# Normalising the queries in channel layout, from two rows that travel through memory, in a gated delta recurrence

## The chip, the cores and the metric

The kernel runs on one core of a Trainium2 chip. The metric is the time of one execution on the device, in microseconds. The profile names the engines PE (matrix products; PEld is its weight load), DVE (VectorE), ACT (ScalarE), POOL (GpSimd) and SP (which here only issues DMAs). The engines run their own instruction streams and meet at semaphores.

## The reference

For 4 sequences of 1024 tokens and 512 features, with 16 heads of 128 channels:

```python
xn = layernorm(x)
q, k, v = xn @ Wq, xn @ Wk, xn @ Wv
beta = sigmoid(xn @ Wb + bb)
q = silu(causal_dwconv(q, qconv_w, qconv_b))      # 4 taps along the tokens
k = silu(causal_dwconv(k, kconv_w, kconv_b))
q = layernorm(q per head, qn_w, qn_b)             # over a head's 128 channels
k = layernorm(k per head, kn_w, kn_b)
S = (1 - b_t) * S + b_t * outer(v_t, k_t)         # for each token t
o_t = S @ q_t
s = (o * silu(xn @ Wg)) @ Wo
g = silu(ffn(xn))                                 # on the 512 tokens of the highest scores, 0 elsewhere
out = x + s * g
```

## The kernel before

Three stages follow each other: the tokens' layer norm and their transposes, the recurrence, and two passes over the kept tokens. The change lies in the recurrence alone, which takes some two thirds of the time.

The recurrence handles one head of one sequence at a time: 64 such units. They run in a software pipeline, in which one *step* of the program does four things: it projects unit A and convolves it, makes q and k of unit B (A's predecessor), finishes q and k of unit C (the one before), and does the chunked recurrence of unit D (the one before that). Tokens are worked in 8 chunks of 128. Each engine's order within a step is written by hand, and every wait is a semaphore with a count. Two steps make a pair (`par` 0 and 1), with small differences: the token ranks of the router are computed in DVE's gaps, one half in each (`rank_greater` in par 0, `rank_ties` in par 1), and the weights of v are loaded once for a pair.

What happens to q of one unit:

1. PE projects it into `ps_proj`, channels on partitions, tokens along the row; ACT (`tap`) and DVE (`convolve`) apply the four taps into `act_cm`; ACT applies silu in place.
2. PE transposes it chunk by chunk (`turn`, 8 transposes, name `QT`), ACT copies it to `tok[0]` with tokens on partitions (`tokens(0)`), and DVE takes the statistics over the channels from there (`statistics(0)`, `variance`). GpSimd raises the variance to the power -1/2, and DVE makes the shift (`shifts`).
3. DVE scales and shifts `tok[0]` (`normalise`: 8 instructions, one for each chunk, since rstd and shift are then one value for each partition). In the next step PE transposes it back (`QB`, 8 transposes), and ACT copies it to `q_cm` with the norm's weight and bias (`ready(0)`).

The keys go the same way, but ACT normalises them, and GpSimd weights them for the state update with two passes over 1024 columns (`k_weighted` and `k_tokens_done`), with q's weighting by the cumulated decay (`q_cum`) between the two. The first of the three waits for `dmat_done`, which DVE's scan over the decays signals. `ps_work` is two PSUM buffers that the transposes (QB, QT, KB, KT), the state updates (UP), the scores (SC) and the outputs (OUT) use in turn. For the first sequence the weights are also split into two parts by ACT and GpSimd; later sequences load the split parts again from memory.

## Time and profile before

| | |
|---|---|
| median of 3 runs | 2653.92 us (2642.51 to 2655.47) |
| the profiled execution | 2649.24 us, its span 2647.5 us |
| busy in the span | PE 2538.9 us, DVE 1779.9 us, ACT 1122.9 us, POOL 849.7 us |
| granted TensorE clock, mean | 0.987 |

An engine's busy time is an average over three stages with different limits, and a busy PE is not PE at its peak. What the change is worth is read from one step in the middle of the recurrence: from the start of an instruction to the start of the same instruction one step on. Each row of the trace gives the start, the duration, the line and the operation with the tiles written and read; a bracket behind it gives the idle time of the engine before it, and who ended it.

### The profile page before, as it was taken

How to read it: one execution, taken by the hardware profiler on the slowest of the kernel's cores; microseconds unless marked ns; L12 is line 12 of the kernel's file. 1: busy time of each engine (PE TensorE's matmuls, PEld its weight loads, DVE VectorE, ACT ScalarE, POOL GpSimd, SP SyncE). 2: the span in 40 equal slices, each digit the busy share in tenths (PEclk: the TensorE clock that was granted, in tenths of full speed). 3: DMA queues.
4: the chain of work that ended last, by engine and by line, in shares of the span. 5: the costliest groups of instructions: out<-in, count | busy, mean ns of one | idle time of the engine just before them, and what ended most of it. 6: DMA issues, size and time to landing. Idle time of an engine off the chain costs nothing. (4 is left out here: it accounts for less than half of the span.)

```text
span 2647.5 us, 44202 instructions
## 1 busy us (share of the span) xinstructions
PE 2538.9 (96%) x15744; PEld 2254.0 (85%) x15744; DVE 1779.9 (67%) x3716; ACT 1122.9 (42%) x1513; POOL 849.7 (32%) x442
## 2 busy tenths in 40 slices
PE   5899999999999999999999999997899999999997
PEld 4789889999999989999998999997788887888886
DVE  5678888888888888888888888888431222433232
ACT  5444454444444444444444444444432323322221
POOL 1245445443434334343434334344100000211220
PEclk8999999999999999999999999999999999999998
DMA  7544443643333353333354333342461101441320
GB/s 273 167 136 153 151 135 128 219 133 104 119 119 119 111 176 125 119 127 104 118 169 134 119 108 122 119 128 80 156 230 49 63 32 56 128 150 48 111 84 27
DMA packets 220876, 327.51 MB, mean 124 GB/s; under 512 B 56310, under 2 KB 156918, under 8 KB 216058
## 3 DMA queue, kind: packets, MB, share of 16 engines
q1 hardware_dynamic: 125946, 192.21, 22.2%
q10 hardware_dynamic: 86144, 109.06, 12.4%
q0 software_dynamic: 8704, 25.19, 3.1%
q8 instruction: 46, 0.75, 0.1%
q14 instruction: 36, 0.29, 0.0%
HBM read 237.77 MB, written 97.03 MB: 126 GB/s over the span
## 5 line engine op out<-in xcount | busy, mean ns | idle before, releaser
L983 DVE SCALAR_TENSOR_TENSOR xn_rows<-ps_proj,conv,xn_rows 128x1021 f32<-128x1021 f32 x381 | 488.0, 1281 | 127.8 <-ACT xn_rows L890 118.7
L1160 PE MATMUL ps_proj<-xt_hi,w_hi 128*128 128x512 f32 x1008 | 411.7, 408 | 20.1 <-DVE xn_rows L983 13.6
L1162 PE MATMUL ps_proj<-xt_hi,w_lo 128*128 128x512 f32 x1008 | 396.8, 394 | 0.0
L1161 PE MATMUL ps_proj<-xt_lo,w_hi 128*128 128x512 f32 x1008 | 395.4, 392 | 0.0
L941 ACT ACTIVATE rc_tok_k<-rc_tok_k,rc_small 128x128 f32<-128x128 f32 x512 | 204.2, 481 | 353.2 <-DVE rc_small L1017 353.2
L782 POOL TENSOR_TENSOR rc_k_state<-rc_tok_k,k_norm_rows 128x1024 f32<-128x1024 f32 x64 | 153.5, 2399 | 515.1 <-issue 397.5
L1182 PE MATMUL ps_proj<-wv_hi,xt_hi 128*128 128x256 f32 x1024 | 294.9, 288 | 0.6 <-PEq L75 0.6
L1183 PE MATMUL ps_proj<-wv_lo,xt_hi 128*128 128x256 f32 x1024 | 289.5, 283 | 0.0
L1184 PE MATMUL ps_proj<-wv_hi,xt_lo 128*128 128x256 f32 x1024 | 289.3, 283 | 0.0
L814 POOL TENSOR_TENSOR rc_small<-rc_small,rc_minus_half 128x16 f32<-128x16 f32 x64 | 187.2, 2924 | 218.9 <-DVE rc_small L1012 218.9
L890 ACT ACTIVATE xn_rows<-ps_proj,conv 128x1024 f32<-128x1024 f32 x127 | 152.9, 1204 | 231.7 <-PE rc_ps_work L1136 231.7
L1160 PEld LDWEIGHTS ps_proj<-xt_hi,w_hi 128*128 128x128 f32 x1008 | 190.6, 189 | 57.3 <-issue 15.2
L1162 PEld LDWEIGHTS ps_proj<-xt_hi,w_lo 128*128 128x128 f32 x1008 | 189.8, 188 | 42.0
L1161 PEld LDWEIGHTS ps_proj<-xt_lo,w_hi 128*128 128x128 f32 x1008 | 190.8, 189 | 35.1
L1586 DVE TENSOR_TENSOR ff_wide_lo<-ff_wide,ff_wide_hi 128x512 fp32r<-128x512 f32 x64 | 44.3, 693 | 245.2 <-ACT ff_wide_hi L1501 245.1
L1247 PE MATMUL rc_ps_work<-rc_v_beta,rc_scores 128*128 128x128 f32 x1024 | 190.6, 278 | 12.2 <-DVE rc_scores L1068 12.1
L1182 PEld LDWEIGHTS ps_proj<-wv_hi,xt_hi 128*128 128x128 f32 x1024 | 196.1, 192 | 1.0 <-issue 1.0
L1183 PEld LDWEIGHTS ps_proj<-wv_lo,xt_hi 128*128 128x128 f32 x1024 | 196.3, 192 | 0.0
L1184 PEld LDWEIGHTS ps_proj<-wv_hi,xt_lo 128*128 128x128 f32 x1024 | 196.0, 191 | 0.0
L1249 PE MATMUL rc_ps_work<-rc_states,rc_q_cum 128*128 128x128 f32 x896 | 175.6, 278 | 0.0
L1582 DVE TENSOR_TENSOR gt_wide<-gt_ps_turn,gt_gate 128x512 f32<-128x512 f32 x64 | 44.2, 691 | 194.2 <-ACT gt_gate L1494 194.2
L991 DVE BATCH_NORM_STATS2 rc_stats<-rc_tok_k 128x6 f32<-128x128 f32 x512 | 105.3, 279 | 100.3 <-ACT rc_tok_k L900 100.3
(177 smaller groups left out, 5770.9 us busy)
## 6 DMA issues: line engine op xcount, KB each, us to landing
rc_decay_all<-scratch_decay ACTq DMA_DIRECT2D x64, 512.0 KB, 3.5
rc_cum_all<-scratch_cum ACTq DMA_DIRECT2D x64, 512.0 KB, 3.6
scratch_o<-rc_o_sb ACTq DMA_DIRECT2D x64, 512.0 KB, 3.2
w_hi<-scratch_w_split SPq DMA_DIRECT2D x48, 512.0 KB, 4.0
w_lo<-scratch_w_split SPq DMA_DIRECT2D x48, 512.0 KB, 4.8
wv_hi<-scratch_wv_split SPq DMA_DIRECT2D x24, 512.0 KB, 3.9
wv_lo<-scratch_wv_split SPq DMA_DIRECT2D x24, 512.0 KB, 4.8
scratch_w_split<-w_hi SPq DMA_DIRECT2D x16, 512.0 KB, 2.8
```

Source lines behind the costliest of these rows:

```text
L782: nc.gpsimd.tensor_tensor(k_tokens[:], tok[1][:], k_norm_rows[:, 0:1].to_broadcast([P, NC, P]), ALU.mult).then_inc(S["k_weighted"], 1)
L814: nc.gpsimd.tensor_tensor(small[:, 6], small[:, 5], minus_half[:], ALU.pow).then_inc(S["rstd_done"], 1)
L941: last = nc.scalar.activation(tok[1][:, c], tok[1][:, c], ACT.Identity, bias=small[:, 7, 1, c:c + 1], scale=small[:, 6, 1, c:c + 1])
L983: nc.vector.scalar_tensor_tensor(out=act_cm[j][:, back:], in0=projected[:, 0:L - back], scalar=conv[par][:, j, t:t + 1], in1=act_cm[j][:, ...
L1160: nc.tensor.matmul(out, hi, xt_hi[:, k, cols], start=k == 0, stop=False)
L1161: nc.tensor.matmul(out, hi, xt_lo[:, k, cols], start=False, stop=False)
L1162: last = nc.tensor.matmul(out, lo, xt_hi[:, k, cols], start=False, stop=k == KC - 1)
L1182: nc.tensor.matmul(out, xt_hi[:, k, cols], wv_hi[:, k], start=k == 0, stop=False)
L1183: nc.tensor.matmul(out, xt_hi[:, k, cols], wv_lo[:, k], start=False, stop=False)
L1184: last = nc.tensor.matmul(out, xt_lo[:, k, cols], wv_hi[:, k], start=False, stop=k == KC - 1)
L1247: last = nc.tensor.matmul(out, scores[:, c], values, start=True, stop=c == 0)
L1249: last = nc.tensor.matmul(out, q_cum[:, c * P:(c + 1) * P], states[:, c - 1], start=False, stop=True)
```

## The change

q is no longer carried through token layout. Its transposes to tokens stay, but only the statistics use them: DVE takes them straight from PSUM, so ACT's copy `tokens(0)`, DVE's `normalise` and PE's transposes back (`QB`) go. In their place, rstd and shift of all 1024 tokens are stored as two rows in memory by ACT, in 4-byte pieces (each partition holds 8 tokens of each row, 128 tokens apart), and loaded back as rows that are repeated on all 128 partitions. The load stands behind the store's completion in ACT's queue. In the next step DVE multiplies q in channel layout by the one row and adds the other (`scale_q`), and `ready(0)` reads that.

```diff
                 if C_.live:
                     after_pair(dve, decay_loaded[C_.par], C_.pair)
                     ...
                     nc.vector.tensor_tensor_scan(dmat[C_.par]...).then_inc(S["dmat_done"], 1)
+                    scale_q()
+                if B_.live:
+                    statistics(0)
                 if A_.live and not first_done(A_.i):
                     convolve(0)
                 if B_.live:
-                    statistics(0)
                     statistics(1)
...
-                def normalise():
-                    after_step(dve, "shift_done", B_.i)
-                    for c in range(NC):
-                        last = nc.vector.tensor_scalar(tok[0][:, c], tok[0][:, c], small[:, 6, 0, c:c + 1],
-                                                       small[:, 7, 0, c:c + 1], ALU.mult, ALU.add)
-                    last.then_inc(S["q_normed"], 1)
+                def scale_q():
+                    after_step(dve, "q_rows_loaded", C_.i, 16)
+                    after_step(dve, "q_turned", C_.i)
+                    nc.vector.tensor_tensor(q_silu[C_.par][:], q_silu[C_.par][:], q_rows[:, 0], ALU.mult
+                                            ).then_inc(S["q_scaled"], 1)
+                    after_step(dve, "q_scaled", C_.i, 2, 1)
+                    nc.vector.tensor_tensor(q_silu[C_.par][:], q_silu[C_.par][:], q_rows[:, 1], ALU.add
+                                            ).then_inc(S["q_scaled"], 1)
...
+                def store_rows():
+                    after_step(act, "rstd_done", B_.i)
+                    after_step(act, "shift_done", B_.i)
+                        act.dma_start(row(scratch["q_rows"], B_.i).rearrange("(k c p) -> p k c", k=2, p=P),
+                                      rstd_shift[:, 0]).then_inc(S["q_rows_stored"], 16)
+                def load_rows():
+                    after_step(act, "q_rows_stored", B_.i, 16)
+                    after_step(act, "q_scaled", B_.i - 1, 2)
+                    act.dma_start(q_rows[:].rearrange("p k t -> p (k t)"),
+                                  row(scratch["q_rows"], B_.i).partition_broadcast(P)
+                                  ).then_inc(S["q_rows_loaded"], 16)
...
                 if B_.live:
-                    after_step(act, "rstd_done", B_.i)
-                    after_step(act, "shift_done", B_.i)
+                    store_rows()
                     for c in range(NC):
-                        last = nc.scalar.activation(tok[1][:, c], tok[1][:, c], ACT.Identity,
+                        last = nc.scalar.activation(tok_k[:, c], tok_k[:, c], ACT.Identity,
                     last.then_inc(S["k_normed"], 1)
+                    load_rows()
...
-                if C_.live:
-                    after_step(pe, "q_normed", C_.i)
-                    after_step(pe, "scores_done", D_.i - 1)
-                    turn(work(par, QB), lambda c: tok[0][:, c]).then_inc(S["q_back"], 1)
...
                     after_step(pe, "k_silu", B_.i)
-                    after_step(pe, "q_tok", B_.i)
+                    after_step(pe, "stats_done", B_.i, 2, 1)
```

With one user of `ps_work` less, the two buffers alternate in a fixed way and the waits between them are rewritten. silu of q goes to a buffer of its own (`q_silu`, two of them). The raw weights of the first sequence share memory with buffers that later stages use, which makes room for the rows.

The two places on which the times turn, as the built programs have them. First DVE, between the end of one step and the statistics of the next, before:

```order
L1023 TENSOR_SCALAR rc_tok_q<-rc_tok_q,rc_small 128x128 x8
L1033 ISA
L1033 TENSOR_TENSOR rc_v_beta<-ps_proj,beta_steps 128x1024
L1044 SCALAR_TENSOR_TENSOR rc_dmat<-rc_decay_all,rc_chunk_ident 128x1024
L622 REGISTER_ALU
L983 SCALAR_TENSOR_TENSOR xn_rows<-ps_proj,conv,xn_rows 128x1021
L622 ISA
L983 SCALAR_TENSOR_TENSOR xn_rows<-ps_proj,conv,xn_rows 128x1022
L622 REGISTER_ALU
L983 SCALAR_TENSOR_TENSOR xn_rows<-ps_proj,conv,xn_rows 128x1023
L991 BN_STATS rc_stats<-rc_tok_q 128x6 x8
L991 BN_STATS rc_stats<-rc_tok_k 128x6 x8
```

The same place of the changed program:

```order
L1056 TENSOR_TENSOR rc_v_beta<-ps_proj,beta_steps 128x1024
L631 REGISTER_ALU
L625 REGISTER_ALU
L1067 SCALAR_TENSOR_TENSOR rc_dmat<-rc_decay_all,rc_chunk_ident 128x1024
L625 ISA
L625 REGISTER_ALU
L1044 TENSOR_TENSOR rc_q_silu<-rc_q_silu,rc_q_rows 128x1024
L625 ISA
L1047 TENSOR_TENSOR rc_q_silu<-rc_q_silu,rc_q_rows 128x1024
L1011 BN_STATS rc_stats<-rc_ps_work 128x6 x8
L625 REGISTER_ALU
L1003 SCALAR_TENSOR_TENSOR xn_rows<-ps_proj,conv,xn_rows 128x1021
```

`normalise` (L1023) is gone from ahead of the gates and the scan (L1044, now L1067); the two passes of `scale_q` stand right behind the scan, and the statistics of q stand ahead of the convolution of q. All of these instructions are in one queue, so a late `q_rows` holds up everything behind it.

Then ACT, from the finished q to the store of the outputs, before:

```order
L880 ACTIVATE rc_q_cm<-rc_ps_work,norm 128x1024
L861 DMA rc_decay_all<-scratch_decay 128x1024
L900 ACTIVATE rc_tok_q<-rc_ps_work 128x1024
L880 ACTIVATE rc_k_cm<-rc_ps_work,norm 128x1024
L867 DMA rc_cum_all<-scratch_cum 128x1024
L900 ACTIVATE rc_tok_k<-rc_ps_work 128x1024
L890 ACTIVATE xn_rows<-ps_proj,conv 128x1024
L941 ACTIVATE rc_tok_k<-rc_tok_k,rc_small 128x128 x8
L947 ACTIVATE rc_o_sb<-rc_ps_work 128x1024
L949 DMA scratch_o<-rc_o_sb 128x8x128
```

and in the changed program:

```order
L884 ACTIVATE rc_q_cm<-rc_q_silu,norm 128x1024
L865 DMA rc_decay_all<-scratch_decay 128x1024
L884 ACTIVATE rc_k_cm<-rc_ps_work,norm 128x1024
L871 DMA rc_cum_all<-scratch_cum 128x1024
L902 ACTIVATE rc_tok_k<-rc_ps_work 128x1024
L894 ACTIVATE xn_rows<-ps_proj,conv 128x1024
L909 DMA scratch_q_rows<-rc_rstd_shift 128x16x1
L960 ACTIVATE rc_tok_k<-rc_tok_k,rc_rstd_shift 128x128 x8
L916 DMA rc_q_rows<-scratch_q_rows 128x2048
L967 ACTIVATE rc_o_sb<-rc_ps_work 128x1024
L969 DMA scratch_o<-rc_o_sb 128x8x128
```

The copy of q's tokens is gone; a store stands ahead of the normalisation of k (L941, now L960) and a load behind it. The evacuation of the outputs (L967) is queued behind the load, which waits for the store.

## Rows read from the trace of the kernel before

**Rows 1.** Busy us and instructions by engine, granted clock, DMA: 400 us of the recurrence

```profile
1200.00:1600.00 400.00, 398.23 (x2769) 364.99 (x2769) 339.15 (x759) 187.91 (x247) 157.97 (x67) 1.00 0.40 129
```

**Rows 2.** Who made PE wait, to 2000 us (longest in the recurrence): total, times, longest

```profile
PE ps_proj L1160 <- DVE xn_rows L983: 13.6, 7, 6.3
```

**Rows 3.** Groups of PE instructions by shape: busy us, mean ns, idle before

```profile
L1136 PE MATMUL rc_ps_work<-ident,rc_tok_q 128*128 128x128 f32 x512 | 66.2, 272 | 1.9 <-DVE rc_tok_q L1023 1.9
```

**Rows 4.** Timeline of PE: the transposes back, what follows, the next step's

```profile
1204.61 1.03 PE L1136 MATMUL rc_ps_work<-ident,rc_tok_q 128*128 128x128 f32 x8
1205.48 1.04 PE L1136 MATMUL rc_ps_work<-ident,xn_rows 128*128 128x128 f32 x8
...
1231.55 1.03 PE L1136 MATMUL rc_ps_work<-ident,rc_tok_q 128*128 128x128 f32 x8
```

**Rows 5.** Timeline of DVE, a little more than one step

```profile
1220.93 0.17 DVE L1017 SCALAR_TENSOR_TENSOR rc_small<-rc_small 128x16 f32<-128x16 f32 x1
...
1227.84 2.19 DVE L1023 TENSOR_SCALAR rc_tok_q<-rc_tok_q,rc_small 128x128 f32<-128x128 f32 x8
1229.95 1.22 DVE L1033 TENSOR_TENSOR rc_v_beta<-ps_proj,beta_steps 128x1024 f32<-128x1024 f32 x1
1231.08 2.28 DVE L1044 TENSOR_TENSOR_SCAN rc_dmat<-rc_decay_all,rc_chunk_ident 128x1024 f32<-128x1024 f32 x1
1234.80 3.92 DVE L983 SCALAR_TENSOR_TENSOR xn_rows<-ps_proj,conv,xn_rows 128x1021 f32<-128x1021 f32 x3 [1.44 <-ACT xn_rows L890]
1238.63 1.64 DVE L991 BATCH_NORM_STATS2 rc_stats<-rc_tok_q 128x6 f32<-128x128 f32 x8
1241.84 1.65 DVE L991 BATCH_NORM_STATS2 rc_stats<-rc_tok_k 128x6 f32<-128x128 f32 x8 [1.57 <-ACT rc_tok_k L900]
...
1247.99 0.17 DVE L1017 SCALAR_TENSOR_TENSOR rc_small<-rc_small 128x16 f32<-128x16 f32 x1
...
1251.90 1.22 DVE L1078 TENSOR_TENSOR rc_k_state<-rc_k_state,rc_dmat 128x1024 f32<-128x1024 f32 x1
...
1254.23 2.14 DVE L1023 TENSOR_SCALAR rc_tok_q<-rc_tok_q,rc_small 128x128 f32<-128x128 f32 x8
```

**Rows 6.** Timeline of POOL in the same step

```profile
1233.59 2.40 POOL L782 TENSOR_TENSOR rc_k_state<-rc_tok_k,k_norm_rows 128x1024 f32<-128x1024 f32 x1 [3.80 <-DVE rc_dmat L1044]
1235.96 2.39 POOL L797 TENSOR_TENSOR rc_q_cum<-rc_q_cm,rc_cum_all 128x1024 f32<-128x1024 f32 x1
1238.32 2.38 POOL L809 TENSOR_TENSOR rc_k_state<-rc_k_state,k_norm_rows 128x1024 f32<-128x1024 f32 x1
```

**Rows 7.** Timeline of ACT in the same step

```profile
1248.25 3.19 ACT L941 ACTIVATE rc_tok_k<-rc_tok_k,rc_small 128x128 f32<-128x128 f32 x8 [5.34 <-DVE rc_small L1017]
```

**Rows 8.** Timeline of DVE and POOL where they meet, first sequence

```profile
317.05 1.51 DVE L1004 TENSOR_TENSOR rc_small<-rc_stats 128x16 f32<-128x16 f32 x1
318.48 2.44 DVE L1005 TENSOR_TENSOR rc_small<-rc_stats 128x16 f32<-128x16 f32 x1
...
316.15 2.37 POOL L805 TENSOR_TENSOR w_lo<-w_raw,w_hi 128x1024 fp32r<-128x1024 f32 x1
318.48 2.39 POOL L809 TENSOR_TENSOR rc_k_state<-rc_k_state,k_norm_rows 128x1024 f32<-128x1024 f32 x1
```

**Rows 9.** DMA issues: count, size of one, median us from issue to landing

```profile
rc_decay_all<-scratch_decay ACTq DMA_DIRECT2D x64, 512.0 KB, 3.5
...
scratch_o<-rc_o_sb ACTq DMA_DIRECT2D x64, 512.0 KB, 3.2
...
wv_hi<-scratch_wv_split SPq DMA_DIRECT2D x24, 512.0 KB, 3.9
...
raw<-scratch_ffn SPq DMA_DIRECT2D x4, 1024.0 KB, 5.7
...
conv<-in_kconv_b SPq DMA_DIRECT2D x64, 0.5 KB, 2.0
...
rc_score_tok<-scratch_score SPq DMA_DIRECT2D x1, 16.0 KB, 5.5
```

More of the change, by code:

```diff
@@ L595, in stage_recurrence @@
         VC = NC // 2
-        QB, QT, KB, KT, UP, SC, OUT = range(7)
+        QT, KB, KT, UP, SC, OUT = range(6)
         class At:
@@ L879, in ready @@
                         after_step(act, "q_cum_done", C_.i - 2)
-                    nc.scalar.activation(out[:], work(par, (QB, KB)[j]), ACT.Identity,
+                    nc.scalar.activation(out[:], source, ACT.Identity,
                                          bias=norm[:, j, 1:2], scale=norm[:, j, 0:1]).then_inc(S[name_out], 1)
@@ L892, in tap, with tokens @@
                                          scale=conv[par][:, j, PAD:TAPS]).then_inc(S[n + "_tap"], 1)
-                def tokens(j):
-                    n = "qk"[j]
-                    after_step(act, n + "_turned", B_.i)
-                    after_step(act, n + "_back", B_.i - 1)
-                    if j == 1:
-                        after_step(act, "k_weighted", B_.i - 1)
-                    nc.scalar.activation(tok[j][:], work(par, (QT, KT)[j]), ACT.Copy).then_inc(S[n + "_tok"], 1)
+                def tokens():
+                    after_step(act, "k_turned", B_.i)
+                    after_step(act, "k_back", B_.i - 1)
+                    after_step(act, "k_weighted", B_.i - 1)
+                    nc.scalar.activation(tok_k[:], work(KT), ACT.Copy).then_inc(S["k_tok"], 1)
+                def store_rows():
+                    after_step(act, "rstd_done", B_.i)
+                    after_step(act, "shift_done", B_.i)
+                    with nc.allow_non_contiguous_dma("one value for each token"):
+                        act.dma_start(row(scratch["q_rows"], B_.i).rearrange("(k c p) -> p k c", k=2, p=P),
[6 more added lines that the diff above has]
+                                  ).then_inc(S["q_rows_loaded"], 16)
                 def silu(j):
@@ L904, in silu @@
                     after_step(act, n + "_conv", B_.i, PAD)
-                    nc.scalar.activation(act_cm[j], act_cm[j], ACT.Silu).then_inc(S[n + "_silu"], 1)
+                    if j == 0:
+                        after_step(act, "q_turned", B_.i - 2)
+                        after_step(act, "q_ready", B_.i - 2)
+                    nc.scalar.activation((q_silu[B_.par][:], act_cm[1])[j], act_cm[j], ACT.Silu
+                                         ).then_inc(S[n + "_silu"], 1)
                 if B_.live:
@@ L918, in step @@
                 if C_.live:
-                    ready(0, "q_back", "q_ready", q_cm[C_.par])
+                    ready(0, "q_scaled", 2, q_silu[C_.par][:], "q_ready", q_cm[C_.par])
                 if B_.live:
                     load_decay(B_.par, B_.i, B_.pair)
-                    tokens(0)
                 if splits(nxt.i, split):
@@ L929, in step @@
                 if C_.live:
-                    ready(1, "k_back", "k_ready", k_cm[C_.par])
+                    ready(1, "k_back", 1, work(KB), "k_ready", k_cm[C_.par])
                     load_cum(C_.par, C_.i, C_.pair)
                 if B_.live:
-                    tokens(1)
+                    tokens()
                 if A_.live:
@@ L964, in _, with work @@
         def _(dve):
-            def work(par, pos):
-                return ps_work[:, (par + pos) % 2]
+            def work(pos):
+                return ps_work[:, pos % 2]
             def chunks(ap):
@@ L1080, in step @@
                                             ).then_inc(S["k_state_done"], 1)
-                last_rank = isinstance(A_.i, int) and A_.i == N - 1
-                if A_.live and not last_rank:
+                if A_.live:
                     (rank_greater, rank_ties)[par](u)
-                if B_.live:
-                    normalise()
-                if last_rank:
-                    rank_ties(u)
             def rank_greater(u):
@@ L1130, in _, with work @@
         def _(pe):
-            def work(par, pos):
-                return ps_work[:, (par + pos) % 2]
+            def work(pos):
+                return ps_work[:, pos % 2]
             def turn(out, source):
@@ L1203, in step @@
                     after_step(pe, "k_normed", C_.i)
-                    after_step(pe, "q_ready", C_.i)
-                    turn(work(par, KB), lambda c: tok[1][:, c]).then_inc(S["k_back"], 1)
+                    if first_done(D_.i):
+                        after_step(pe, "k_ready", 0)
+                    after_step(pe, "outputs_done", D_.i - 1)
+                    turn(work(KB), lambda c: tok_k[:, c]).then_inc(S["k_back"], 1)
                 if A_.live and not first_done(A_.i):
@@ L1244, in step @@
                     for c in range(NC):
-                        out = work(par, OUT)[:, c * P:(c + 1) * P]
+                        out = work(OUT)[:, c * P:(c + 1) * P]
                         values = v_beta[D_.pair_par][:, c, D_.par]
```

76 lines of the change are left out of this document (43 added, 33 removed).

## The prediction

> **What bounds the kernel now.** I read the windows first: in the middle of the recurrence PE is busy in 398.2 of 400 us at the full granted clock, DVE in 339.2, ACT in 187.9, POOL in 158.0 [rows 1]. Then the waits of PE: the longest entry of the recurrence adds up to 13.6 us, and the transposes back of q waited 1.9 us in 64 steps [rows 2, 3]. So PE sets the pace, and a step is 1231.55 - 1204.61 = 26.94 us [rows 4]. Then the timelines of the other engines, to see how far behind PE they are. DVE is the near one. Its step runs from one `shifts` (L1017) to the next, 1247.99 - 1220.93 = 27.06 us, and two idle places stand in it: 1.44 us before the convolution of q, waiting for ACT's tap, and 1.57 us before the statistics of k, waiting for ACT's copy [rows 5]. DVE is thus a few us short of being the bound itself, and the sum below has to be made for both engines.
>
> **PE, what goes.** Eight transposes a step. Their busy time of 66.2 us for 512 [rows 3] counts overlaps, so I take the distance in start from the first group of eight to the next: 1205.48 - 1204.61 = 0.87 us [rows 4]. Nothing else is removed from PE or added to it. PE alone would come to 26.94 - 0.87 = 26.07 us a step, 64 x 0.87 = 55.7 us in all.
>
> **DVE, what goes and comes.** `normalise` goes: 1229.95 - 1227.84 = 2.11 us. The two passes of `scale_q` come, each a product or sum of two SBUF tensors of 128x1024; the same form is L1078 at 1.22 us, so 2.44 us [rows 5]. The statistics of q read PSUM in place of SBUF; DVE's passes over PSUM and SBUF of one size have the same 1.22 us here (L1033, L1078), so I leave 1.64 us [rows 5]. ACT's copy of q's tokens goes and two DMA issues come; ACT is busy in less than half of its time [rows 1], so that is nothing, as long as its queue is not held up (below).
>
> **DVE against POOL.** This is the cost that the diff doesn't show. The scan signals `dmat_done`, which releases POOL's weighting of k: POOL starts at 1233.59, 0.23 us after the scan's end (1231.08 + 2.28 = 1233.36), and has three passes of 2.4 us in a row, up to 1240.70 [rows 5, 6]. Before, DVE had nothing in that stretch but an idle place, convolutions and statistics. Now both passes of `scale_q` fall into it. What such a meeting costs is in the trace of the first sequence: L1004, a DVE operation of two SBUF tensors of only 16 columns, started at 317.05 while POOL's L805 ran (316.15 to 318.52) and ended at 318.56; L1005 behind it took 2.44 us and ended with POOL's next pass, L809 (318.48 to 320.87) [rows 8]. So a DVE operation with two SBUF inputs waits until POOL's running pass is over, then one gets through, and POOL's next pass has the turn. The convolutions, with one input in PSUM, go on beside POOL: 3.92 us [rows 5].
>
> The Trainium skill says the same in *SBUF — State Buffer*, section "Who interferes with whom": a DVE instruction with two SBUF inputs contends with a GpSimd instruction that reads SBUF, and the one that issues second is blocked until the first is finished. The rows agree. Without the rule and the rows one would book 2.44 us for `scale_q` and end at PE's bound, 55.7 us faster.
>
> Who comes first behind the scan then matters. If the rows of q have landed, DVE's first pass starts at once (its instructions follow each other without a gap), 0.23 us ahead of POOL. The second pass waits for the first by semaphore, and POOL's weighting takes the turn between: 1.22 + 2.40 + 1.22 = 4.84 us. If the rows land after the scan's end, the weighting is first, then pass one, then `q_cum`, then pass two: another 2.40 us, 7.24 us.
>
> DVE's step in the first case: from `shifts` to the gates without `normalise` 1227.84 - 1220.93 = 6.91 us (par 1) or 1254.23 - 1247.99 = 6.24 (par 0); gates and scan 1233.36 - 1229.95 = 3.41; `scale_q` 4.84; statistics of q 1.64; convolution of q 1238.63 - 1234.80 = 3.83; from the statistics of k to `shifts` 1247.99 - 1241.84 = 6.15 [rows 5]. Sums: 26.78 and 26.11, mean 26.45 us. The two idle places are then used up. This is above PE's 26.07, so DVE becomes the bound by a little, and the step gains 26.94 - 26.45 = 0.49 us, not 0.87. In the second case the mean is 28.85 us, a loss of 1.91 us a step.
>
> **When the rows land.** From `shifts` to the scan's end DVE needs 6.91 + 3.41 = 10.32 us (par 1) or 9.65 us (par 0). In this time: ACT wakes (1248.25 - 1247.99 = 0.26 us [rows 5, 7]), the store lands, ACT issues the load, the load lands. The normalisation of k, 3.19 us [rows 7], stands between the issues and is covered by the store. The trace has no store in 4-byte pieces. From below: 128 such pieces loaded, 2.0 us. From above: 4096 such pieces loaded, 5.5 us. The changed one has 2048, stored to memory; I take 3.2 us, which `scratch_o` needs (1024 pieces of 512 bytes, also a store by ACT), and which lies between the two. For the load, 512 KB repeated on all partitions take 3.5 us, 1024 KB from memory 5.7 us; the load is of 1024 KB, I take 5.7 [rows 9]. Sum 0.26 + 3.2 + 5.7 = 9.16 us: 0.49 us before the scan's end in par 0, 1.16 us in par 1. With 3.5 for the load it is 6.96; with the store at 5.5, 11.46, after the scan in both.
>
> The Trainium skill, *DMA: Bandwidth & Descriptors*, section "Specifications", says that below 512 B the DMA engines read, modify and write, which speaks against this store. No run here shows what that costs for 2048 pieces.
>
> **ACT's queue.** The load waits for the store, and the evacuation of the outputs and the silus of the next step are queued behind it. With the store landed 3.46 us after `shifts`, about when the normalisation of k is through, nothing is held up; each us more that the store needs goes to DVE's wait first.
>
> **Sum.** 64 x 0.49 = 31 us. At the end of the recurrence no other unit covers the way through memory, 8.9 us in place of 2.11; the finishing of k runs beside it, so I take 3 us of the 6.8. The profiled execution took 2649.24 us for a span of 2647.5; 2649.24 - 31 + 3 = 2621. The median of the runs is 4.7 us above the profiled execution, inside their spread (2642.5 to 2655.5). I forecast **2621 us**.
>
> **Rivals.**
> - *The rows land late in both halves of a pair*: the store's price above 3.7 us decides (0.49 us more in par 0), above 4.4 in par 1. Then 28.85 us a step, 64 x 1.91 = 122 us slower, 2774. For it: the margin is small, and 4-byte stores are unmeasured. Against: 4096 pieces in 5.5 us leave 0.9 ns for a piece above the 2.0, so 2048 would be at 3.8 or less by reading.
> - *Late in one half only*: in one step of a pair the weights of v are loaded meanwhile, twice 512 KB at 3.9 us on the same DMA engines [rows 9], which can cost the load its margin. Then (26.45 + 28.85) / 2 = 27.65, 0.71 x 64 = 45 us slower, 2697.
> - *No meeting worth naming, PE stays the bound*: if DVE's second pass starts before POOL gets its turn, DVE's mean is 24.05 us, and the step PE's 26.07: 2649.24 - 55.7 = 2594. Against it stand L1004 and L1005.
> - *Nothing moves*: the rows are in time, but DVE, without idle time left, passes each delay on, and the 0.49 us is eaten: within 0.5% of before.
>
> **Chances.** First case as forecast 0.53, PE's bound 0.07, nothing moves 0.1, one half late 0.15, both late 0.15. A range that leaves out the last, and a little of PE's bound: 2592 to 2697; the forecast's own is 2603 to 2636. 0.5%, about 13 us, is what a measurement of this kernel can tell from no change. Faster 0.57, within it 0.12, slower 0.31.
>
> **What would show it.** Right: 512 transposes fewer on PE, steps of about 26.5 us, DVE without idle places, the second pass of `scale_q` some 3.6 us long and the first 1.2, PE with short waits for DVE. Wrong: the first pass long too, or DVE idle for the load ahead of it (rows late); both passes at 1.2 us (no meeting); the store's landing far from 3.2 us or the load's from 5.7 us; PE waiting for the statistics of q before the transposes of k.

## The result, and the profile after

The changed kernel took 3095.95 us (median of 4 runs, 3088.64 to 3098.35); the kernel before, measured beside it, 2654.69 us. The ratio is 1.1666, with a 95% interval of 1.1621 to 1.171. The forecast was 2621 us, its range 2592 to 2697. The profiled execution has a span of 3086.8 us.

First the same 400 us of the recurrence as in [rows 1]: length, then busy us and instructions of PE, PEld, DVE, ACT and POOL, the granted clock, DMA share and GB/s.

```profile
1200.00:1600.00 400.00, 338.71 (x2144) 304.29 (x2145) 282.95 (x537) 141.86 (x192) 128.52 (x54) 0.91 0.44 127
```

No engine is busy all the time any more: PE has 338.7 us where it had 398.2. So something is waited for. PE's granted clock is 0.91 in the mean here, in place of 1.00: about once a step it falls to half for 3 to 10 us, behind idle time of PE. The waits up to 2400 us (engine and line, who ended the wait; us in all, times, longest):

```profile
ACT rc_o_sb L967 <- DMA scratch_q_rows<-rc_rstd_shift: 511.7, 62, 11.1
DVE rc_q_silu L1044 <- DMA rc_q_rows<-scratch_q_rows: 438.6, 56, 11.9
ACT rc_q_cm L884 <- DVE rc_q_silu L1047: 292.1, 64, 9.3
PE rc_ps_work L1156 <- ACT rc_q_silu L926: 274.7, 60, 8.8
...
DVE rc_v_beta L1056 <- issue: 123.5, 12, 12.6
```

Read them as a chain. ACT stands 511.7 us until the store of the rows has landed. DVE stands 438.6 us in front of `scale_q`. What depends on DVE and ACT, down to PE's transposes of q, waits in turn. The last row is of another kind, a wait for nothing that the profile shows; it comes back below.

One step of it, ACT's timeline (start, duration; the bracket is the idle time ahead and who ended it):

```profile
1422.25 0.41 ACTq L909 DMA_DIRECT2D scratch_q_rows<-rc_rstd_shift  x1
1422.71 3.19 ACT L960 ACTIVATE rc_tok_k<-rc_tok_k,rc_rstd_shift 128x128 f32<-128x128 f32 x8 [5.84 <-DVE rc_rstd_shift L1037]
1433.93 0.37 ACTq L916 DMA_DIRECT2D rc_q_rows<-scratch_q_rows  x1
1434.43 1.02 ACT L967 ACTIVATE rc_o_sb<-rc_ps_work 128x1024 f32<-128x1024 f32 x1 [8.54 <-DMA scratch_q_rows<-rc_rstd_shift]
```

The store is issued at 1422.25, the load that waits for it at 1433.93: 11.7 us, where the forecast had 3.2. Over the 64 steps this distance is 10.6 to 14.3 us. The DMA engines had taken all packets of this store by 1424.5; its completion came 9 us later. Other transfers are held up meanwhile. On SP's queue one issue of 0.5 KB took 7.18 us in this stretch, and these transfers land late (KB each, median us from issue to landing):

```profile
rc_q_rows<-scratch_q_rows ACTq DMA_DIRECT2D x64, 1024.0 KB, 6.9
...
scratch_o<-rc_o_sb ACTq DMA_DIRECT2D x64, 512.0 KB, 6.4
...
wv_hi<-scratch_wv_split SPq DMA_DIRECT2D x24, 512.0 KB, 12.8
```

The output store had 3.2 us before, the weights of v 3.9 [rows 9].

DVE, in two successive steps of the changed kernel (`L1138` is the last instruction of a pair of steps):

```profile
1428.65 0.21 DVE L1138 TENSOR_SCALAR rc_token_id<-rc_token_col,rc_first_slot 128x1 int32 x1
1440.05 1.22 DVE L1056 TENSOR_TENSOR rc_v_beta<-ps_proj,beta_steps 128x1024 f32<-128x1024 f32 x1 [11.19 <-issue]
1441.19 2.28 DVE L1067 TENSOR_TENSOR_SCAN rc_dmat<-rc_decay_all,rc_chunk_ident 128x1024 f32<-128x1024 f32 x1
1443.39 1.20 DVE L1044 TENSOR_TENSOR rc_q_silu<-rc_q_silu,rc_q_rows 128x1024 f32<-128x1024 f32 x1
1444.62 3.28 DVE L1047 TENSOR_TENSOR rc_q_silu<-rc_q_silu,rc_q_rows 128x1024 f32<-128x1024 f32 x1
...
1466.73 2.28 DVE L1067 TENSOR_TENSOR_SCAN rc_dmat<-rc_decay_all,rc_chunk_ident 128x1024 f32<-128x1024 f32 x1
1475.91 1.27 DVE L1044 TENSOR_TENSOR rc_q_silu<-rc_q_silu,rc_q_rows 128x1024 f32<-128x1024 f32 x1 [6.90 <-DMA rc_q_rows<-scratch_q_rows]
1477.22 1.23 DVE L1047 TENSOR_TENSOR rc_q_silu<-rc_q_silu,rc_q_rows 128x1024 f32<-128x1024 f32 x1
```

In the second step the first pass starts 6.90 us after the scan's end, when the rows have landed. In the first step they are in time, but only since DVE stood still for 11.19 us ahead of the scan; there the second pass takes 3.28 us. POOL beside that first step:

```profile
1443.81 3.01 POOL L785 TENSOR_TENSOR rc_k_state<-rc_tok_k,k_norm_rows 128x1024 f32<-128x1024 f32 x1 [13.10 <-DVE rc_dmat L1067]
1446.78 3.39 POOL L800 TENSOR_TENSOR rc_q_cum<-rc_q_cm,rc_cum_all 128x1024 f32<-128x1024 f32 x1
```

A pause like the 11.19 us turns up in each fourth step of the later sequences, and four steps are one turn of their loop. It lies between the loop's backward branch and the next instruction that DVE executes. One of the two queues that bring code to the engines fetched more than before; here its row of the DMA queues (packets, MB, share of time), of the changed kernel and then of the kernel before:

```profile
q14 instruction: 86, 0.70, 0.1%
```

```profile
q14 instruction: 36, 0.29, 0.0%
```

Two things were thus to be told apart: the price of the store in small pieces, and a pause of DVE at the branch that the forecast doesn't have.

### The profile page after: what moved, and what is told of

The parts are those of the page before. It is cut to its first block and busy times, and to the rows that moved or that the text cites. A ratio compares the mean times of both kernels' runs of the same rounds, so it can differ in the third digit from the quotient of the medians.

```text
span 3086.8 us, 43386 instructions
## 1 busy us (share of the span) xinstructions
PE 2640.0 (86%) x15232; PEld 2309.8 (75%) x15232; DVE 1821.5 (59%) x3332; ACT 1061.6 (34%) x1449; POOL 865.0 (28%) x442
## 5 line engine op out<-in xcount | busy, mean ns | idle before, releaser
L1180 PE MATMUL ps_proj<-xt_hi,w_hi 128*128 128x512 f32 x1008 | 453.1, 449 | 58.4 <-DMA xt_lo<-scratch_xt_lo 29.1
L1003 DVE SCALAR_TENSOR_TENSOR xn_rows<-ps_proj,conv,xn_rows 128x1021 f32<-128x1021 f32 x381 | 486.4, 1277 | 11.6 <-ACT xn_rows L894 2.5
L1181 PE MATMUL ps_proj<-xt_lo,w_hi 128*128 128x512 f32 x1008 | 428.1, 425 | 0.0
L1182 PE MATMUL ps_proj<-xt_hi,w_lo 128*128 128x512 f32 x1008 | 424.8, 421 | 0.0
L1156 PE MATMUL rc_ps_work<-ident,rc_q_silu 128*128 128x128 f32 x512 | 117.2, 404 | 274.7 <-ACT rc_q_silu L926 274.7
L1044 DVE TENSOR_TENSOR rc_q_silu<-rc_q_silu,rc_q_rows 128x1024 f32<-128x1024 f32 x64 | 87.3, 1364 | 438.6 <-DMA rc_q_rows<-scratch_q_rows 438.6
L960 ACT ACTIVATE rc_tok_k<-rc_tok_k,rc_rstd_shift 128x128 f32<-128x128 f32 x512 | 204.0, 481 | 400.3 <-DVE rc_rstd_shift L1037 400.3
L818 POOL TENSOR_TENSOR rc_rstd_shift<-rc_small,rc_minus_half 128x16 f32<-128x16 f32 x64 | 187.0, 2923 | 545.6 <-DVE rc_small L1031 545.6
L1156 PEld LDWEIGHTS rc_ps_work<-ident,rc_q_silu 128*128 128x128 f32 x512 | 93.3, 210 | 300.3 <-ACT rc_q_silu L926 181.6
L1180 PEld LDWEIGHTS ps_proj<-xt_hi,w_hi 128*128 128x128 f32 x1008 | 216.5, 215 | 107.2 <-DMA xt_lo<-scratch_xt_lo 30.4
L967 ACT ACTIVATE rc_o_sb<-rc_ps_work 128x1024 f32<-128x1024 f32 x64 | 65.5, 1023 | 523.4 <-DMA scratch_q_rows<-rc_rstd_shift 511.7
```

The lines of the kernel that those rows point to most:

```text
L818: nc.gpsimd.tensor_tensor(rstd_shift[:, :, 0], small[:, 5], minus_half[:], ALU.pow).then_inc(S["rstd_done"], 1)
L960: last = nc.scalar.activation(tok_k[:, c], tok_k[:, c], ACT.Identity, bias=rstd_shift[:, 1, 1, c:c + 1], scale=rstd_shift[:, 1, 0, c:c + 1])
L1003: nc.vector.scalar_tensor_tensor(out=act_cm[j][:, back:], in0=projected[:, 0:L - back], scalar=conv[par][:, j, t:t + 1], in1=act_cm[j][:, ...
L1156: last = nc.tensor.transpose(out[:, c * P:(c + 1) * P], source(c), ident[:])
L1180: nc.tensor.matmul(out, hi, xt_hi[:, k, cols], start=k == 0, stop=False)
L1181: nc.tensor.matmul(out, hi, xt_lo[:, k, cols], start=False, stop=False)
```

## The experiments

### What the store costs

**Pieces of 64 bytes.** Each partition's 16 values go out as one piece, and the rows come back in the order of the partitions, so q is scaled by values of other tokens; all the work is the same.

```diff
-... row(scratch["q_rows"], B_.i).rearrange("(k c p) -> p k c", k=2, p=P), rstd_shift[:, 0] ...
+... row(scratch["q_rows"], B_.i).rearrange("(p f) -> p f", p=P), rstd_shift[:, 0].rearrange("p k c -> p (k c)") ...
```

> The store of rstd and shift writes the same 8 KB in 128 pieces of 64 bytes (each partition's 16 values together), so the rows that come back hold the values in another order and q is scaled by wrong values; every instruction, wait and load is as in the changed kernel. Theory 'pieces' (the 11.5 us that the store took in the changed kernel come from its 2048 pieces of 4 bytes, and all of the loss follows from them): store to load issue about 3.5 us after the store's issue, and the time that the prediction summed for rows in time, 2621 us, between 2600 and 2660. Rival 'queues' (the loss comes from the longer ACT queue and from 1 MB more to load in a step): above 2850 us.

Measured: 2681.92 us, ratio 1.0121 [1.01, 1.0141]. The store's row among the DMA issues:

```profile
scratch_q_rows<-rc_rstd_shift ACTq DMA_DIRECT2D x64, 8.0 KB, 1.4
```

The same 8 KB land in 1.4 us in most steps, ACT's wait for the store falls from 511.7 to 9.6 us and DVE's for the rows from 438.6 to 9.5. 414 of the 441 us lost are the price of the small pieces, with all that follows from it. What is left is 30 us above before, where the forecast had a gain. In the later sequences the excess is in each fourth step: 32.4 us from scan to scan, beside 25.5 to 26.3 in the others.

**Pairs of 8 bytes.** rstd and shift of a token stand next to each other: 1024 pieces. The two passes then read every second value of the rows.

```diff
-rstd_shift = sb("rstd_shift", [P, 2, 2, NC])
+rstd_shift = sb("rstd_shift", [P, 2, NC, 2])
...
-... row(scratch["q_rows"], B_.i).rearrange("(k c p) -> p k c", k=2, p=P) ...
+... row(scratch["q_rows"], B_.i).rearrange("(c p k) -> p c k", k=2, p=P) ...
...
```

> rstd and shift of a token lie side by side in memory, so the store has 1024 pieces of 8 bytes; the multiply and the add read every second element; the result is the reference's. Theory 'pieces': the landing falls with the count, (11.5 - 2) / 2 + 2 = 6.8 us from store to load, the rows land about 3 us after the scan, a step takes 29 to 31 us, 2780 to 2900 us in all. Rival 'bytes or a fixed price of a store that a load waits for': 11 us and 3050 to 3100 us as before.

Measured: 2826.96 us, one run. The store mostly lands in 4.3 to 5.4 us in one half of a pair and in 6.7 to 10.6 us in the other, where the weights of v are loaded; its median:

```profile
scratch_q_rows<-rc_rstd_shift ACTq DMA_DIRECT2D x64, 8.0 KB, 5.3
```

**2048 pieces, 64 bytes apart.** The 4-byte pieces of the change, each with 60 unused bytes behind it. The load reads 8 KB of the input x in their place, so q is scaled by other values.

```diff
-... row(scratch["q_rows"], B_.i).rearrange("(k c p) -> p k c", k=2, p=P) ...
+... row(scratch["q_spread"], B_.i).rearrange("(k c p) s -> p k c s", k=2, p=P)[:, :, :, 0] ...
...
```

> 2048 pieces of 4 bytes as in the changed kernel, but each goes to a 64-byte line of its own; the load reads 8 KB of the input x instead (initialised memory of the same size and form), so q is scaled by wrong values. Theory 'pieces' (a piece costs what it costs wherever it goes): store to load 10.7 to 12 us, 3050 to 3130 us. Rival 'lines' (16 pieces to one 64-byte line hold each other up): 3 to 5 us, and 2600 to 2720 us.

Measured: 2801.32 us, one run; the store lands after 3.6 to 5.1 us in one half of a pair, mostly 7 to 9 in the other. Its median:

```profile
scratch_q_spread<-rc_rstd_shift ACTq DMA_DIRECT2D x64, 8.0 KB, 5.0
```

The landing is the one that the rival 'lines' had, the time is above its 2720 us, since the rows still come late in the other half. In the undisturbed half the same number of equally small pieces needs less than half of the time when they don't lie next to each other. So neighbouring pieces hold each other up. But 3.6 us and more are not yet the 1.4 of the 64-byte pieces: the number of the pieces, or their size, counts besides, and these runs don't tell the two apart.

**The store alone.** The kernel before, with rstd and shift also stored in 4-byte pieces. Nobody loads them or waits for them, except the next step's writers of the same buffer, and ACT once at the end of the recurrence.

```diff
+                        act.dma_start(row(scratch["q_rows"], B_.i).rearrange("(k c p) -> p k c", k=2, p=P),
+                                      rstd_shift[:, 0]).then_inc(S["q_rows_stored"], 16)
```

> The kernel before with nothing changed but the store of 2048 pieces of 4 bytes in each step, issued by ACT ahead of the normalisation of k; nobody loads the rows, and only the next step's rstd and shift wait for it. Theory 'pieces, and the way through memory is waited for': a step of 26.9 us covers 11.5 us, so 2650 to 2700 us, though loads that fall into the store's time land late (the weights of v 12 us in place of 3.9). Rival 'contention' (the DMA engines, held up by the store, are the loss, and not the wait for the rows): over 2850 us.

Measured: 2688.28 us, ratio 1.0138 [1.0121, 1.0155]. The store lands after 11 us or more here too (12.4 in the median), and the output store behind it and the weights of v late (3.2 and 3.9 us before [rows 9]):

```profile
scratch_o<-rc_o_sb ACTq DMA_DIRECT2D x64, 512.0 KB, 11.5
...
wv_hi<-scratch_wv_split SPq DMA_DIRECT2D x24, 512.0 KB, 14.0
```

The steps keep their length except at four places, three of them where a sequence begins and the tokens are loaded (35 to 40 us in place of 27 to 31). So the traffic by itself costs some 35 us here. That the rest of the 414 is waiting for the store follows only if the traffic costs no more in the changed kernel; the next run and the steps of the trace speak for it.

**The load out of ACT's way.** In the changed kernel the load is issued behind the next step's q tap, ahead of `ready(0)`, so that ACT's queue goes on while the store is under way.

```diff
                     last.then_inc(S["k_normed"], 1)
-                    load_rows()
...
                 if C_.live:
+                    load_rows()   # of C_.i
                     ready(0, "q_scaled", 2, q_silu[C_.par][:], "q_ready", q_cm[C_.par])
```

> The changed kernel with the load of the rows issued behind ScalarE's q tap of the next step instead of behind the normalisation of k, so that ScalarE's queue does not stand still while the store is under way. Theory 1 (what costs is that the rows come late to VectorE, which does nothing else meanwhile; ScalarE's standing still, 511 us of waits, lies beside it): steps stay at 32 to 34 us, 3060 to 3110. Theory 2 (ScalarE's held queue costs as much by itself, since the output copy, the silus and the taps of the next step stand behind the wait): steps fall by 3 us or more, below 2950.

Measured: 3189.87 us, one run. ACT's 511.7 us of waits are gone from the list and nothing is gained: DVE waits longer for the rows than in the changed kernel (438.6 us):

```profile
DVE rc_q_silu L1044 <- DMA rc_q_rows<-scratch_q_rows: 582.5, 58, 20.1
```

The time is above both expectations; the store took 11.5 to 12.9 us in most steps, about 1 us more than in the changed kernel's trace, as the next part shows. The direction speaks for the first theory: late rows cost, the standing queue lies beside it.

One step of the changed kernel's own trace shows it too, from `shifts` (L1037) over the store (L909), the load (L916) and the two passes above (1475.91 to 1478.45) to the next `shifts` and store:

```profile
1459.36 0.16 DVE L1037 SCALAR_TENSOR_TENSOR rc_rstd_shift<-rc_small,rc_rstd_shift 128x16 f32<-128x16 f32 x1
1459.73 0.41 ACTq L909 DMA_DIRECT2D scratch_q_rows<-rc_rstd_shift  x1
1470.71 0.34 ACTq L916 DMA_DIRECT2D rc_q_rows<-scratch_q_rows  x1
...
1490.97 0.16 DVE L1037 SCALAR_TENSOR_TENSOR rc_rstd_shift<-rc_small,rc_rstd_shift 128x16 f32<-128x16 f32 x1
1491.35 0.41 ACTq L909 DMA_DIRECT2D scratch_q_rows<-rc_rstd_shift  x1
```

From one store to the next these are 11.0 us for the store, 5.2 for the load, 2.5 for the passes, 12.5 from there to the next `shifts` (DVE's statistics and convolutions, POOL's power) and 0.4 until ACT issues: 31.6 us, one step. So the way through memory has become a closed loop that sets the step. With the 64-byte store and no pause the same legs come to some 23 us (1.5 for the store), less than PE needs, and DVE waits for no rows in most of the later steps. The leg up to `shifts` takes 12.2 us in the mean of the changed kernel's later steps and 11.5 there, so an estimate of what PE's lower clock can have added to the loop is 0.7 us a step at most.

### The pause at the branch

**The loop moved.** The 64-byte kernel, with 60 semaphore increments that nobody waits for at the head of DVE's recurrence program, so that its loops stand 60 instructions further on.

```diff
+            for _ in range(60):
+                stand(dve, keep["carrier_dve"])
             steps(dve, step, first_kept_rows)
```

> The kernel of the 64-byte store (q still scaled by wrong values, since the rows keep that store's order), with 60 semaphore increments that nobody waits for at the head of VectorE's program of the recurrence: its loop of four steps then begins 60 instructions later in the instruction stream, and nothing else changes. In that kernel VectorE executes nothing for 5.4 to 6.1 us after each of the loop's ten backward branches, 8 KB pieces of code are fetched then, and each fourth step takes 32.4 us beside 25.5 to 26.3. Theory (where the loop stands decides whether the beginning of it is still there at the branch): the next instruction follows the branch by 0.1 us, the extra fetches of code inside the loop are gone, each fourth step falls to 25.5 to 26.5, the time falls by about 10 times 6.5 us to 2610 to 2625, less up to 6 us for the increments themselves. Rival (the body is too long, or ScalarE's longer program, 186 instructions in four steps where it had 158, is what is fetched): the gaps and the time stay, 2675 to 2690.

Measured: 2640.15 us, ratio 0.9958 [0.9944, 0.9973]. DVE at the branch and the fetched code, first without the increments:

```profile
1189.78 0.21 DVE L1138 TENSOR_SCALAR rc_token_id<-rc_token_col,rc_first_slot 128x1 int32 x1
1195.63 1.23 DVE L1056 TENSOR_TENSOR rc_v_beta<-ps_proj,beta_steps 128x1024 f32<-128x1024 f32 x1 [5.64 <-issue]
```

```profile
q14 instruction: 87, 0.70, 0.1%
```

and with them:

```profile
1168.34 0.21 DVE L1138 TENSOR_SCALAR rc_token_id<-rc_token_col,rc_first_slot 128x1 int32 x1
1169.05 1.22 DVE L1056 TENSOR_TENSOR rc_v_beta<-ps_proj,beta_steps 128x1024 f32<-128x1024 f32 x1 [0.50 <-issue]
```

```profile
q14 instruction: 31, 0.25, 0.0%
```

The pause is gone with code that does nothing. I had expected 2610 to 2625: the fourth step falls to 27.0 us, not 26, and the steps of the first sequence are no shorter than in the kernel before (392 us for 14 of them, 390 before).

**The loop of the kernel before moved**, by 100 such increments.

> The kernel before with 100 such increments at the head of VectorE's program of the recurrence, nothing else. Theory that the place of the loop decides: here the gap appears, 5 to 6 us of VectorE after each backward branch of the second loop, with four or five fetches of 8 KB in each turn of it, where before had none between 617 and 1718 us, although the body of the loop is the same to the instruction. What it costs in time is less than the gap, since VectorE is busy 339 of 400 us there and TensorE sets the step: 10 to 40 us, so 2665 to 2700. Rival (the change's own body or its additional instructions on other engines cause it): no gap, no fetches, 2645 to 2665.

Measured: 2668.57 us, ratio 1.0065 [1.0042, 1.0089]. The unchanged loop now shows the same fetches, and a pause in each turn (waits of DVE from 500 to 2000 us):

```profile
DVE rc_v_beta L1033 <- issue: 27.3, 10, 4.6
```

So where the loop stands decides, not what it holds: 315 instructions a turn before, 305 after. Only two places were tried for each; at which of them a loop does well in general is not shown. The pause costs little here. Of the 17.8 us between the two traces, 8.6 lie ahead of the first scan, where the increments themselves stand, and only 5.5 in the 45 later steps with the pauses, where PE and not DVE is busy all the time [rows 1]. The pause is also shorter, 2.7 us each, since the eight instructions of `normalise`, already handed to DVE, run on into it. The Trainium skill, *Runtime: NRT & Kernel Launch*, section "Instruction fetch mechanics", has the rule: a taken branch to code that the engine no longer holds must fetch it first. The runs agree, with 5.4 to 6.1 us for a branch in the 64-byte kernel; the pieces fetched on this queue are of 8192 bytes, the page's blocks are of 16 KiB.

**The changed kernel with its loop moved**, by the same 60 increments.

> The changed kernel (2048 pieces of 4 B) with the 60 increments at the head of VectorE's recurrence program, nothing else. In the changed kernel VectorE executes nothing for 10.6 to 12.3 us after each of ten backward branches, and the steps there read 44 and then 25.5, where the others are 32.4 to 34. Theory (the gap is the loop's place, and half of it is given back since the rows come in time in the step behind it): no gap, all steps at 32 to 34 us, and since 44 + 25.5 is 4 us more than two such steps, 11 times 4 is 45 us less: 3035 to 3065. Rival (the gap is the store's doing, which holds up everything then, fetched code or not): 3085 to 3105.

Measured: 3131.65 us, 36 above the changed kernel, although the pause was gone. Neither theory had that. But the store landed 1.1 us later in the mean than in the changed kernel's trace, in 60 of the 64 steps, in the first sequence too. So both were measured on one chip:

> The changed kernel itself, beside the one with the moved loop on one chip. If the store's length differs between chips, it lands here at the same 11.6 to 12.7 us as in that kernel, and the time is 3120 to 3180. If it is the moved loop that lengthens the store, it lands at 10.7 to 11.6 us again, and the time is 3085 to 3105.

> The changed kernel with the moved loop, once more. Theory (the pause at the branch is given back in part, since the rows come in time in the step behind it: 44 and 25.5 us for two steps of 32.5 to 34): 0 to 45 us below the changed kernel on the same chip, with the store of the same length in both. Rival (moving the loop costs by itself): 20 us or more above it.

Measured: the changed kernel 3094.35 us, with its loop moved 3054.13, the store alike in both (mostly 10.5 to 11.9 us). The pause costs 40 us here too. What is known to have differed before is the chip: the same kernel took 3131.65 us on one and 3054.13 on another, with the 4-byte store about 1 us longer on the first, while the medians of the kernel before lie within 4 us of each other wherever it was measured. Why the store differs stays open.

### What bounds it when the rows are in time

**The rows read in steps of 64 bytes.** The 64-byte store and the moved loop; DVE reads the rows in the order of the store.

```diff
-q_rows = sb("q_rows", [P, 2, L])
+q_rows = sb("q_rows", [P, P, 2, NC])
...
-nc.vector.tensor_tensor(q_silu[C_.par][:], q_silu[C_.par][:], q_rows[:, 0], ALU.mult ...
+nc.vector.tensor_tensor(chunks(q_silu[C_.par][:]), chunks(q_silu[C_.par][:]),
+                        q_rows[:, :, 0].rearrange("p t c -> p c t"), ALU.mult ...
...
```

> The 64-byte store and the moved loop, and VectorE reads the loaded rows in the order in which they were stored (a step of 16 values, 64 bytes, between the values of neighbouring tokens), so that all of the reference's work is done. Theory (VectorE reads such steps at the same pace): pass one 1.20 us, the time as that of the kernel with the moved loop, 2600 to 2630. Rival (steps of 64 bytes halve the pace of the two passes): pass one 2.4 us, VectorE becomes the bound by 1.2 to 2.4 us in a step, 2680 to 2780.

Measured: 2727.44 us, ratio 1.029 [1.027, 1.0309]. The passes take 1.9 and 4.0 us, which is the rival in kind:

```profile
1223.64 1.95 DVE L1044 TENSOR_TENSOR rc_q_silu<-rc_q_silu,rc_q_rows 128x1024 f32<-128x1024 f32 x1
1225.62 4.03 DVE L1047 TENSOR_TENSOR rc_q_silu<-rc_q_silu,rc_q_rows 128x1024 f32<-128x1024 f32 x1
```

**POOL's weighting behind the second pass**, in that kernel and then in the one that reads in straight order.

```diff
-                    after_step(pool, "dmat_done", C_.i)
+                    after_step(pool, "q_scaled", C_.i, 2)
```

> As the one before it, and GpSimd's weighting of k is released by the second pass over q instead of the scan. Both theories expect the second pass at 1.2 us instead of 3.3 and the weighting's first half no longer beside it. Theory (TensorE is the bound once rows come in time: it is busy 25.6 of 25.6 us in such steps and VectorE 24.7 to 25.1): the steps stay at 25.5 to 26.3, the time within 10 us of the kernel with the weighting released by the scan. Rival (VectorE is the bound at 25.8, as the forecast had it): the steps fall by 1 to 2 us and the time by 50 to 100.

> The 64-byte store read in straight order (q scaled by wrong values), the loop moved, and GpSimd's weighting of k released by the second pass over q instead of the scan. Both theories expect the second pass at 1.2 us instead of 3.3. Theory (TensorE is the bound as soon as rows come in time, busy 131.4 of 131.4 us in five steps of the kernel without this edit, where VectorE has 126.7): the step stays at 26.3 in the mean and the time within 8 us of that kernel's 2640, so 2632 to 2645. Rival (VectorE is the bound, as the forecast put it at 26.45 with TensorE at 26.07): 2.1 us less on VectorE gives at least 0.4 us a step back, 2615 or less.

Measured: 2643.08 us, 84 less than with the scan's release; and 2622.51 us, ratio 0.9884 [0.9865, 0.9904], 18 less. In the first, the turn of four steps falls from 110.0 to 104.4 us although PE's work is the same: with the scan's release DVE was the bound (386.1 us of 400 busy, PE 385.4), so my theory of PE as the bound didn't hold there. In the second, the time lies between both expectations. The turn of four steps stays at 104.4 us to the tenth although each second pass fell from 3.3 to 1.2 us: PE bounds the later sequences. In the two traces, which are 11.6 us apart, the gain lies in the first sequence, in the steps at which a sequence begins and in the last steps of the recurrence.

**Each eighth token.** As the last one, with q's transposes on every eighth token: a partition then holds eight neighbouring tokens. Once with 64-byte pieces and rows read in runs of 32 bytes, once with 256 pieces of 32 bytes and rows read straight.

```diff
-turn(work(QT), lambda c: q_silu[B_.par][:, c * P:(c + 1) * P]) ...
+turn(work(QT), lambda c: q_silu[B_.par][:].rearrange("p (t c) -> p t c", c=NC)[:, :, c]) ...
...
-... row(scratch["q_rows"], B_.i).rearrange("(k c p) -> p k c", k=2, p=P) ...      # 32-byte pieces
+... row(scratch["q_rows"], B_.i).rearrange("(k p c) -> p k c", k=2, p=P) ...
```

> As the one before it, with all of the reference's work done: TensorE's transposes of q take each eighth token (a step of 32 bytes between the columns read), so that the rows lie in memory in runs of eight tokens that VectorE reads as they come. Theory (runs of 32 bytes are read at full pace by both engines): passes 1.2 us each, eight transposes 1.0 us as before, the time as that of the kernel before it, 2630 to 2645. Rival 1 (VectorE's pace falls with the gaps between the runs): passes of 1.5 to 1.9 us as with single values in steps of 64 bytes, no change in time while TensorE is the bound, up to 2660. Rival 2 (TensorE reads columns in steps of 32 bytes more slowly): the eight transposes take 2 us or more, 64 times 1 us, 2700.

> The kernel of the eighths with the rows stored in 256 pieces of 32 bytes in their natural order, read in straight order; all of the reference's work is done. Theory 1 (what counts is how many pieces there are: 128 pieces land in 1.4 us, 1024 in 4.5 to 5): 256 pieces land in 1.6 to 2.2 us in an undisturbed step, rows in time, 2615 to 2635. Theory 2 (every piece that shares a 64-byte line with another pays, whatever their number): 4 us or more, rows late in part of the steps, 2680 or more.

Measured: 2622.30 us, ratio 0.9889 [0.9869, 0.9909], and 2620.76 us, ratio 0.9886 [0.987, 0.9903]. Both do all of the reference's work and beat both kernels, the one before by 1.1%. Two pieces in each 64 bytes cost little: the store lands after 1.6 us in place of 1.4. The 32-byte version: the store's landing, then 400 us by engine, then DVE and POOL in a step.

```profile
scratch_q_rows<-rc_rstd_shift ACTq DMA_DIRECT2D x64, 8.0 KB, 1.6
```

```profile
1200.00:1600.00 400.00, 399.31 (x2759) 366.73 (x2758) 355.95 (x686) 182.81 (x248) 160.98 (x69) 1.00 0.53 171
```

```profile
1213.28 1.20 DVE L1044 TENSOR_TENSOR rc_q_silu<-rc_q_silu,rc_q_rows 128x1024 f32<-128x1024 f32 x1
1214.51 1.22 DVE L1047 TENSOR_TENSOR rc_q_silu<-rc_q_silu,rc_q_rows 128x1024 f32<-128x1024 f32 x1
...
1215.90 2.39 POOL L785 TENSOR_TENSOR rc_k_state<-rc_tok_k,k_norm_rows 128x1024 f32<-128x1024 f32 x1 [4.18 <-DVE rc_q_silu L1047]
```

PE is full again, 399.3 of 400 us, and the two passes and POOL's weighting follow each other.

## Why the prediction was wrong

- **The store's price: the step that failed.** The forecast took 3.2 us, with 5.5 as the upper bound. It is 10.6 to 14.3 us, no less with nobody waiting for it, and 1.4 to 1.6 us in 128 or 256 pieces where no weights are loaded beside it. The bounds came from loads of small pieces and from a store of 512-byte pieces; neither is a row of stores of small neighbouring pieces. With the store at 11 us the way through memory is longer than PE's step and sets the step at 32 to 34 us. The sentence on the Trainium skill's rule for transfers under 512 B (*DMA: Bandwidth & Descriptors*, "Specifications") pointed the right way and carried no weight; by itself it doesn't give the price either, since pieces of 64 and 32 bytes are under 512 too and land in 1.4 and 1.6 us.
- **Rows late in both halves** was the rival that came true, in kind. Its 2774 us was too low for the same reason: it priced what a late start does between DVE and POOL (2.4 us a step) and left out that the rows could come 7 to 9 us after the scan.
- **The load** was put at 5.7 us: 6.9 in the changed kernel, 4.8 to 5.1 with pieces of 64 and 32 bytes. Right in size.
- **ACT's queue** does stand still, as the forecast feared, but in the one run in which it goes on nothing is gained, and the closed loop accounts for the step without it.
- **DVE against POOL** was right in kind: 1.20 us, then a second pass of 3.28 us that ends 1.1 us after POOL's first pass (4.48 for both where 4.84 were forecast). POOL's first pass, which started 0.8 us before the end of DVE's first, grows from 2.4 to 3.0 us, and its second, beside the end of DVE's second, to 3.4: each side waits for the other in turn, which the forecast booked for DVE alone. The Trainium skill's rule on two SBUF inputs (*SBUF — State Buffer*, "Who interferes with whom") agrees. With the weighting released later both passes take 1.2 us. When the rows are late by 7 us, POOL is through before, and the passes take 1.27 and 1.23 us; the 7.24 us of that case never occurred in the changed kernel. Where rows came only a little late, in the first sequence of the 64-byte kernel and in the 8-byte one, both passes took up to 6.75 us.
- **DVE as the new bound** at 26.45 us was at least 0.35 us too high: with the meeting in place and no pause the later sequences run at 104.4 / 4 = 26.1 us a step. That is the 26.07 forecast for PE alone, so the term of 0.87 us is right.
- **The pause at the branch** was in no part of the forecast: 40 us in the changed kernel.
- **The sum.** 3096 us, less 414 for the pieces, less 42 for the loop's place, less 18 for POOL's release, comes to 2622. These are the differences of kernels measured one after the other, so the sum must come out for the last of them. What it does show is that the two last kernels, which have edits of all three kinds and scale q by the right values, measure the same: 2622 and 2621. That the forecast was 2621 as well is luck: the kernel that it describes, with rows in time in most steps and POOL released by the scan (the 64-byte pieces with the loop moved), measured 2640.
- **The gain that is left.** 0.85 us x 64 = 54 would have been more than the 31 gained. In the trace of the 32-byte kernel the 45 later steps give 39.7 us; the steps of the first sequence stay at 28 us, as before, and from the last scan to the end it takes 5.9 us more, where the forecast had 3. Why the first sequence gains nothing was not followed further; the store lands after 4 to 5 us in every second step there, and POOL and ACT also split weights.

## What to carry to other kernels

A way through memory is priced by the size and the neighbourhood of its pieces: give each partition a run of neighbouring values, here by choosing which tokens a transpose takes, before counting what the way saves. A bound must come from rows of the same kind; without a store of such pieces in the trace the upper bound was open, and the range should have been too. The way has to be added up as a loop, from one store to the next: here it cost nothing as long as it stayed below the 26 us in which PE makes a step, and what lay above was lost. And when a change shows a regular pause with no releaser behind a loop's branch, look at the fetched code and move the loop by a few idle instructions before blaming the change: the loop of the kernel before had been well placed by chance.

## What the runs showed of the hardware

- 2048 neighbouring 4-byte pieces (8 KB) to memory: 10.6 to 14.3 us, though in an undisturbed step the packets were taken within 1.3 us; in the undisturbed half also, 64 bytes apart 3.6 to 5.1; 1024 of 8 bytes 4.3 to 5.4; 256 of 32 bytes 1.6; 128 of 64 bytes 1.4. Beside weight loads the last two took 3 to 5.5. With the 4-byte store alone added, 512 KB loads issued meanwhile on another queue went from 3.9 to 14.0 us.
- The same loop of DVE fetched no code at one place, and five pieces of 8 KB a turn at another, with 5.4 to 6.1 us lost at each branch, and 10.6 to 12.3 us when the 4-byte store was under way.
- A DVE pass of two SBUF inputs took 1.93 us with single values 64 bytes apart, 1.20 us with runs of 32 bytes. PE's transposes of columns 32 bytes apart took 274 and 276 ns each in the two kernels, those of neighbouring columns beside them 272 (all in the later sequences).
